# Layer 0 of a four-layer graph network: the chain that makes a group's weights runs at other positions of the edge loop

## The reference, cut to what matters

```python
h = einsum('nf,fhd->nhd', x, W)
a_src = sum(h * att_src, axis=-1)
a_dst = sum(h * att_dst, axis=-1)
e = leaky_relu(a_src[src] + a_dst[dst], 0.2)
e_max = segment_max(e, dst)
e_exp = exp(e - e_max[dst])
denom = segment_sum(e_exp, dst)
alpha = e_exp / (denom[dst] + 1e-16)
out = relu(segment_sum(h[src] * alpha, dst) + bias)
```

## Time and profile before

| what | value |
|---|---|
| median of three runs | 5997.77 us |
| the profiled execution | 6000.81 us, its span 5999.0 us |
| layer 0, first gather to last addition | 131.9 to 1286.4 us |
| its groups, first to last weights | 170.1 to 1271.3 us, 51 steps from group to group |
| TensorE's granted clock over the kernel | 0.753 |

### The profile page before, as it was taken

The page is one execution under the profiler, slowest core; times in us unless marked ns, Lnnn a source line. Parts: engine busy times, 40 slices in busy tenths (PEclk is TensorE's granted clock), DMA queues, the critical chain, the costliest instruction groups (busy, mean ns, idle before and its releaser), DMA issues.

```text
span 5999.0 us, 80569 instructions
## 1 busy us (share of the span) xinstructions
PE 4283.5 (71%) x13320; PEld 2473.3 (41%) x13320; DVE 3532.0 (59%) x10770; ACT 2587.1 (43%) x7522; POOL 4048.5 (67%) x4116
## 2 busy tenths in 40 slices
PE   5798989855777777977777752777777756666662
PEld 3566766632333333643333321333333623333331
DVE  4677677883333334833333347666666667777777
ACT  1555565645444443444444452000000466666664
POOL 2777677736777775057777775777777377777772
PEclk8878787876767678977777765776777877777776
DMA  4333333323333332033333322333333122222221
GB/s 128 106 106 105 93 104 99 106 92 120 106 105 105 106 106 79 31 99 105 106 106 105 106 81 84 106 105 106 105 106 105 52 53 53 53 53 53 53 53 54
DMA packets 237711, 539.69 MB, mean 90 GB/s; under 512 B 68266, under 2 KB 120424, under 8 KB 237242
## 3 DMA queue, kind: packets, MB, share of 16 engines
q0 software_dynamic: 180176, 481.36, 29.1%
q1 hardware_dynamic: 57066, 53.19, 2.7%
HBM read 498.15 MB, written 36.14 MB: 89 GB/s over the span
## 4 chain that ended last, share of the span: by engine, by line
PE 41%; DMA 16%; issue 13%; DVE 12%; POOL 11%; ACT 5%; DVEq 1%; SPq 0%; ACTq 0%; POOLq 0%
PE bank L1153 18%; DMA scratch<-tab_x,src_idx 10%; PE bank L1549 10%; POOL scratch L1121 9%; PE bank L971 7%; DMA scratch<-tab_h,src_idx 5%; PE bank L828 4%; PE bank L816 2%; DVE reg_acc L1175 1%; DVE scratch L185 1%; DVE scratch L203 1%; DVE reg_acc L999 1%; POOL reg_x L724 1%; ACT scratch L1564 1%; DVE scratch L1265 1%
## 5 line engine op out<-in xcount | busy, mean ns | idle before, releaser
L1153 PE MATMUL bank<-scratch 128*128 x4980 | 2215.7, 567 | 953.1 <-SPq L1128 605.9
L1175 DVE TENSOR_TENSOR reg_acc<-reg_acc,bank 128x256 f32 x2490 | 1048.9, 421 | 1691.2 <-PE bank L1153 1659.9
L1153 PEld LDWEIGHTS bank<-scratch 128*128 128x128 f32 x4980 | 1093.8, 260 | 2074.4 <-issue 2004.7
L1121 POOL DMA_INDIRECT scratch<-tab_x,src_idx x1564 | 1483.5, 949 | 514.3 <-issue 277.4
L1134 ACT ACTIVATE scratch<-iota_row,dst_loc 128x128 f32<-128x128 f32 x1660 | 661.2, 400 | 1024.2 <-PE bank L1153 1004.1
L1121 POOL DMA_INDIRECT scratch<-tab_h,src_idx x782 | 741.1, 948 | 462.1 <-DMA tab_h<-reg_acc 224.0
L1522 POOL DMA_INDIRECT scratch<-tab_h,src_idx x832 | 856.3, 1029 | 263.8 <-issue 157.3
L724 POOL DMA_INDIRECT reg_x<-tab_h,src_idx x832 | 813.3, 978 | 297.6 <-issue 176.8
L1549 PE MATMUL bank<-scratch 128*128 128x260 f32 x1664 | 674.3, 522 | 429.2 <-issue 402.2
L971 PE MATMUL bank<-reg_x,scratch 128*128 128x265 f32 x1664 | 637.5, 492 | 100.7 <-DVE reg_x L1008 68.5
L1549 PEld LDWEIGHTS bank<-scratch 128*128 128x128 f32 x1664 | 325.3, 241 | 746.5 <-issue 708.2
(11 more groups left out here) (230 smaller groups left out, 4423.8 us busy)
## 6 DMA issues: line engine op xcount, KB each, us to landing
scratch<-tab_h,src_idx POOLq DMA_INDIRECT x1614, 2.7
scratch<-tab_x,src_idx POOLq DMA_INDIRECT x1564, 2.7
reg_x<-tab_h,src_idx POOLq DMA_INDIRECT x832
reg_x<-in_x SPq DMA_DIRECT2D x12, 896.0 KB, 11.0
tab_h<-scratch SPq DMA_DIRECT2D x7, 924.0 KB, 4.5
tab_x<-reg_acc SPq DMA_DIRECT2D x7, 896.0 KB
tab_h<-reg_acc SPq DMA_DIRECT2D x7, 896.0 KB
tab_x<-reg_x SPq DMA_DIRECT2D x7, 896.0 KB
```

Of the source, the lines that this page charges most:

```text
L1121: e.indirect_dma_start(ring_rows[:, j % SLOTS, :], None, self.table, bass.IndirectOffsetOnAxis(ap=src_idx[:, j:j + 1], axis=0)).then_inc(* ...
L1153: e.matmul(psum[i % EDGE_BANKS][:, 0:FEAT], ring_hots[:, i % HOTS, :], rows, start=True, stop=True).then_inc(*self.product.up)
L1175: e.tensor_tensor(v, v, psum[i % EDGE_BANKS][:, 0:FEAT], ALU.add).then_inc(*self.added.up)
```

## The change

The work is the same, and its pieces stand at other positions. On ScalarE the one-hots are made four at a time, all of a quarter in one piece, at k 0, 2, 4 and 5. The copy of the masks (`step_masks`) moves from k 0 to k 3, `part` from behind to ahead of `shrink` (k 11 to k 10). On TensorE the one-hots are turned at 1, 3, 5 and 6 (before 2, 4, 6 and 8) and the destination scores multiplied at 3, 5, 7 and 8 (before 4, 6, 8 and 10). VectorE takes the scores at 13 instead of 12.

```diff
         def chain_scalar(e, g, k, ahead):
-            def distance(n):
-                for t in (g * S + n, g * S + n + 1):
-                    if g >= 2:
-                        e.wait_ge(*product0(t - 2 * S))
+            def hot(c):
+                a = (g * S + 4 * c) % (2 * S)
+                if g >= 2:
+                    e.wait_ge(*product0(g * S + 4 * c + 3 - 2 * S))
+                for t in range(g * S + 4 * c, g * S + 4 * c + 4):
                     e.activation(hots0[:, t % (2 * S), :], iota_row[:, :], ACT.Abs, scale=-1.0,
                                  bias=dst_loc[:, t:t + 1]).then_inc(*far0.up)
-
-            def hot(c):
-                a = (g * S + 4 * c) % (2 * S)
                 e.wait_ge(*far0(g * S + 4 * c + 3))
...
                 if k == 0:
                     if g:
+                        e.wait_ge(*ch_t.at("turned3", g - 1))
+                    e.copy(upright[:, 0:2 * P].rearrange("p (k s h) -> p k s h", k=2, h=H),
+                           bcast(masks[:, :, cols], 3, [P, 2, S, H])).then_inc(*ch_a.done("upright"))
+                if k in (0, 2, 4, 5):
+                    hot((0, 2, 4, 5).index(k))
+                if k == 3:
+                    if g:
                         e.wait_ge(*ch_v.at("level_out", g - 1))
                     e.copy(step_masks.rearrange("p (k h s) -> p k h s", k=2, h=H),
                            bcast(run_masks[:, :, cols], 2, [1, 2, H, S])).then_inc(*ch_a.done("step_masks"))
-                    if g:
-                        e.wait_ge(*ch_v.at("part_added", g - 1))
-                    e.copy(upright[:, 0:2 * P].rearrange("p (k s h) -> p k s h", k=2, h=H),
-                           bcast(masks[:, :, cols], 3, [P, 2, S, H])).then_inc(*ch_a.done("upright"))
...
-                if k < 8:
-                    distance(2 * k)
-                if k in (1, 3, 5, 7):
-                    hot(k // 2)
+                if k == 10:
+                    e.wait_ge(*ch_t.at("dst3", g))
+                    if g:
+                        e.wait_ge(*ch_v.at("larger_added", g - 1))
+                    e.copy(dst_part, bank_d[:, 0:S * H]).then_inc(*ch_a.done("part"))
                 if k == 11:
                     e.wait_ge(*ch_v.at("below_node", g))
                     e.activation(shrink0, shrink0, ACT.Exp).then_inc(*ch_a.done("shrink"))
-                    e.wait_ge(*ch_t.at("dst3", g))
-                    e.copy(dst_part, bank_d[:, 0:S * H]).then_inc(*ch_a.done("part"))
...
                 keep_hot(2)
-            if k == 8:
+            if k == 7:
                 keep_hot(3)
 
         def chain_tensor(e, g, k, ahead):
...
-            if k == 2:
+            if k == 1:
                 turn_hots(0)
-            if k == 4:
+            if k == 3:
                 turn_hots(1)
                 dst_scores(0)
-            if k == 6:
+            if k == 5:
                 turn_hots(2)
                 dst_scores(1)
+            if k == 6:
+                turn_hots(3)
             if k == 7:
...
+                dst_scores(2)
             if k == 8:
-                turn_hots(3)
-                dst_scores(2)
-            if k == 10:
                 dst_scores(3)
...
         def chain_vector(e, g, k):
...
-            if k == 12:
+            if k == 13:
                 e.wait_ge(*ch_a.at("part", g))
                 e.tensor_tensor(both[:, 0:P], upright[:, 2 * P:3 * P], dst_part,
                                 ALU.add).then_inc(*ch_v.done("part_added"))
-            if k == 13:
                 e.wait_ge(*ch_t.at("larger", g))
```

More of the change, by code:

```diff
@@ L704, in build @@
         ch_t = s_chain["tensor"].named(
-            "turned3 hots0 tails hots1 dst0 hots2 dst1 begins hots3 dst2 dst3 larger", GROUPS)
+            "turned3 hots0 hots1 dst0 tails hots2 dst1 hots3 begins dst2 dst3 larger", GROUPS)
         ch_a = s_chain["scalar"].named(
-            "step_masks upright hot0 kept3 kept_hot0 hot1 kept_tails kept_hot1 hot2 begins kept_hot2 hot3 begin_col "
-            "kept_hot3 shrink part weights", GROUPS)
+            "upright hot0 kept3 hot1 kept_hot0 step_masks hot2 kept_tails kept_hot1 hot3 begins kept_hot2 kept_hot3 "
+            "begin_col part shrink weights", GROUPS)
         far0 = s_far.take(STEPS_PAD)
```

## The result

The changed kernel takes 5933.71 us (median of 4 runs, 5929.54 to 5935.68), the one before beside it 5995.85 us (4 runs, 5970.04 to 6015.3). The ratio is 0.9897, interval 0.9871 to 0.9922: 1% faster. The profiled execution took 5935.68 us with a span of 5933.9; the one of before had 6000.8 and 5999.0.

A forecast was written before the change was run, and what follows sets the result against it. Gathers and compute engines were taken to limit layer 0 by turns, gathers alone after the change. Terms -32.0 and -15.4 sum to -47.4; 3 given back makes -44, 6000.8 to 5956.8, put at 5956 us, range 5943 to 5993.

The forecast's parts named there:

- a new wait of L892: On VectorE at k 6, waiting for ScalarE's kept tails (L793): some 0.5 us a group.
- the gathers' pace: GpSimd's issue in layer 0: 1.29 us a gather, so the last starts at 1203.9 instead of 1235.9, -32.0 us.
- the drain: Layer 0 behind its last gather: 35.2 us instead of 50.6, so -15.4.
- the rest of the kernel: Everything outside layer 0: taken as in the profiled execution of 6000.8 us, with no change.
- bound by the gathers: Likeliest case, layer 0: GpSimd's issue sets the pace throughout, -35 to -50 us, 52%.
- The fast group: A layer 0 group at granted clock 1.00: 1.2 us shorter, 17.3 us instead of 18.5.
- The slow group: A layer 0 group at low TensorE clock: 22.4 us instead of 24.6, with 40% of groups slow.
- TensorE's shorter list behind the product of step 4: Second quarter's transposes, tile-number load and first scores move ahead of that product: 1.99 us off the loop, 1.14 net.
- Port contention: VectorE and GpSimd sharing a port pair: another 0.02 us on each gather, pace 1.31, forecast -28; the rows did not bear it out.
- Slower: Rival: TensorE's clock falls in 65% of groups, mean 22.0 us a group, +23 us, 6024; 13%.
- the wait moves: Rival: L931's wait goes to the larger scan and L892, the loop keeps its length, 5993 to 6003 us; 13%.
- Part of the gain only: Rival: compute engines stay the limit from 350 us on, a group gains 0.5 us, -25, 5976 us; 22%.

The follow-up runs named there:

- b_extra_products: The kernel before with the product of step 3 computed twice more in every group; 5939.49 us against 5989.98, ratio 0.9924.
- a_extra_vector: The changed kernel with four unneeded 128x128 additions on VectorE per group behind L877; 5937.24 us, ratio 0.9922 to the kernel before.
- b_scores_at_13_again: The kernel before with only VectorE's scores moved from 12 to 13; 5939.07 us against 5989.98, ratio 0.9917.
- a_half_gathers: The changed kernel with every second gather of layer 0 left out from step 48 on; 20.17 us a group.
- a12_half_gathers: The changed kernel with VectorE's scores back at 12 and every second gather of layer 0 left out from step 48 on; 20.89 us a group.

## Why the prediction was right or wrong

*Which engine binds.* Right for the profiled execution: GpSimd throughout, L931's wait gone, L877 waiting, no gather held, a new wait of L892. Other edits that take the compute engines below the gathers (b_extra_products, a_extra_vector, b_scores_at_13_again) end at 1062.7 to 1068.9 us of gathers, near the 1062.7 of the change.

*What failed.* The mechanism held and the sum was too small. Three of its terms were mis-sized, by 9.0, 3.9 and 7.8 us: the gathers' pace, taken as 1.29 us where 1.279 was measured, the drain, and the rest of the kernel, taken as unchanged. The first is the largest, and the other two put the time outside the range.

*The gathers' pace.* 9.0 us, the largest miss. The two stretches of the earlier trace rows gave 1.293 and 1.274 us, and I took 1.29 because the first stretch "was bound by the gathers". Measured: 1.279, within the bounds. The gathers of the first stretch lasted 0.990 us each, those of the second 0.970, and after the change they last 0.974 (810.5 / 832) with a pause of 0.305. The first stretch was short, and one gather more or less among its 138 moves its pace by 0.009 us. The last gather came at 1194.9 instead of 1203.9.

*The drain.* 34.3 us measured, 35.2 counted. The count was right; the 3 us I gave back for a slow group at the end were not needed. Together 3.9 us.

*The rest of the kernel.* Taken over as it stood in the one profiled execution of before, that is, priced at nothing. 7.8 us of the difference between the two profiled executions lie there, because that execution was slower outside layer 0 than the five later ones (4713.1 us behind the last addition, the five 4701.4 to 4705.3). With 9.0, 3.9, 7.8 and 0.4 of rounding the 21.1 us between -44 and -65.1 are accounted for.

*The range.* This is the step that put the time outside. Its lower end, 5943, is the sum with the pace of 1.274 and the 3 us given back: 6000.8 - 45.3 - 15.4 + 3 = 5943.1. The gathers came 4.3 us later than that end has them, so the pace did not break it. The drain (3.9) and the rest of the kernel (7.8) did: 5943.1 + 4.3 - 3.9 - 7.8 = 5935.7, the profiled time. The end had room for the pace and none for those two. The prediction also gave its likeliest case, bound by the gathers, as -35 to -50, where its own two paces give -42 to -58.

*The fast group.* Predicted 17.3, measured 17.5 where the gathers leave it free (a_half_gathers). Right, and so is what it was derived from, as the single groups show.

*The slow group and how many there are.* Predicted 22.4 and 40%, mean 19.3. Measured 23.8 and 9 of 51, but with 26 middle groups of 20.45, a kind that the prediction did not have; the mean is 20.17. I read two single groups and made two kinds of them. That the clock would fall about as often was right. Here it did no harm, since 20.17 is still below 20.46, but of the 1.3 us of margin that I counted 0.3 were there: that the gain came in full was in part luck. The wait of L892 is 0.85 us instead of 0.5, since the tails stand behind the first scores on TensorE and ScalarE waits for them too (19.1 us), which I had ScalarE pass without a wait.

*What carries the gain.* The prediction derived it from TensorE's shorter list behind the product of step 4. For the length of a group at a given clock the runs agree: that part alone takes a fast group from 18.37 to 17.48 us, as both together do (17.47), and VectorE's move alone to 17.91. But the timed gain needs only that the mean falls below the gathers' 20.46, and for that VectorE's move alone was enough (19.31, and 5939.07 us in the timed runs), which the prediction had not seen. The TensorE and ScalarE part alone had 20.89 us in its one execution; the difference to both together lies in the number of slow groups, and what decides that number was not tried.

*Port contention.* The Trainium skill, page "SBUF — State Buffer", section "Who interferes with whom", has VectorE and GpSimd share a port pair; the prediction held that a busier VectorE would by that rule lengthen the gathers and bring the forecast to -28. The 208 added VectorE instructions left the gathers at 810.6 us, so no run here shows it. The section in fact says that such additions contend with GpSimd's reads but, by its own inference, not with what a gather needs; the trace agrees with that. What does lengthen single gathers, to up to 1.2 us, is open.

*The rivals.* "Slower" and "the wait moves" fell: the time fell by 1%, and the slow groups became fewer, not more. "Part of the gain only" is nearer the truth than the result shows. The compute engines gained 1.2 us a group, not 2.3, and had the gathers come a little faster it would have been the case (argued from one execution each, not run).

## What to carry to other kernels

Where two things limit a loop by turns, measure each by itself: half of the feeder's work left out gave the compute engines' own pace in one run, and it showed that a margin argued as 1.3 us was 0.3. Any edit that brings the slower side below the other then gives the same gain, so ask for the smallest: here one move on VectorE did what the whole change did. Where the clock varies, compare groups at the same granted clock as well as the means. A forecast of 1% also needs a share for what one execution of the same kernel differs from the next. And when TensorE shows a granted clock below 1 while it waits for others, try giving it redundant work there before reordering anything.

## What the runs showed of the hardware

- Redundant products made a kernel faster. Two more per group raised the granted clock from 0.82 to 0.97 (350 to 550 us) and the whole kernel gained 0.8%.
- GpSimd's issue of one 128-row gather costs 0.946 us (median) and a pause of 0.30 us that stands before every gather, waiting or not; with the longer ones among them it is 1.279 to 1.286 us a gather in the profiles of the changed kernel, of VectorE's move alone, of the extra products and of the extra additions.
- A granted clock is not set by the order alone: the same changed kernel had 0.92 in one profile and 0.79 to 0.83 in another over the same stretches, with the same work.
- TensorE's granted clock was 0.80 over 975 us in which its matmuls were busy for 889 and no idle stretch was longer than 1.0 us (a12_half_gathers).
- In some series every kernel took some 18% longer, with pauses of up to 7 us behind no signal of the kernel. The cause is open.
